# Router transposes placed behind ready products, and batch 1's preparation for the last feed-forward placed after the attention core

## The reference, cut to what matters

```python
x = x + _L0_xattn_ref(_layernorm(x), ctx_1024, ...)      # attention-free mixer, layer norm, MLP 256-1024-256, layer norm
x = x + _L0_ffn_ref(_layernorm(x), ...)                  # mixture of 64 experts, 8 per token, and 2 shared MLPs
x = x + _L1_xattn_ref(_layernorm(x), ctx_1024, ...)      # masked softmax attention, 16 heads of 16
x = x + _L1_ffn_ref(_layernorm(x), ...)                  # gelu MLP with sign weights times a mean magnitude

# inside _L0_ffn_ref
probs = jax.nn.softmax(xf @ router_w + router_b, axis=-1)
tw, ti = jax.lax.top_k(probs, K)
tw = tw / jnp.sum(tw, axis=-1, keepdims=True)
h = jax.nn.silu(xf @ W1 + B1) @ W2 + B2                  # for every expert, weighted by its tw
# inside _L1_ffn_ref, bw = alpha * sign(w)
h = jax.nn.gelu(jnp.einsum('bsd,hd->bsh', x, bw1) + b1, approximate=False)
out = jnp.einsum('bsh,dh->bsd', h, bw2) + b2
```

## Time and profile before

| | |
|---|---|
| median of 3 runs | 1220.96 us (1219.16 to 1221.37) |
| the profiled execution's own time | 1220.14 us |
| its span | 1218.15 us |
| PE busy | 1132.7 us, 93% |
| DVE busy | 885.5 us, 73% |
| ACT busy | 704.4 us, 58% |
| POOL busy | 348.0 us, 29% |
| chain that ended last, by engine | PE 27%, DVE 7%, issue 4%, ACT 3% |

### The profile page before, as it was taken

One profiled execution on the slowest core, in us unless ns is written; L12 is line 12 of the kernel. 1 busy time (PEld: TensorE's weight loads), 2 busy tenths in 40 slices (PEclk: granted clock), 3 DMA queues, 4 the chain that ended last, 5 costly groups with the idle time before them and its releaser, 6 DMA issues. The chain is left out here.

```text
span 1218.1 us, 19950 instructions
## 1 busy us (share of the span) xinstructions
PE 1132.7 (93%) x6928; PEld 987.9 (81%) x6928; DVE 885.5 (73%) x1656; ACT 704.4 (58%) x1066; POOL 348.0 (29%) x343
## 2 busy tenths in 40 slices
PE   4889998988889999999999999999999999989998
PEld 3678887877779999999999888788788788777877
DVE  6888859766756556556554445999999989998575
ACT  2233334665534444444443155988988988987755
POOL 1613211622614204204100074412613522333120
PEclk9999999998999999999999999999999999999999
DMA  9200000043334342343220032322321432310011
GB/s 326 69 1 1 1 1 2 11 133 74 66 103 127 112 138 101 110 137 103 95 93 3 6 110 78 110 86 64 109 75 54 135 108 75 98 41 7 13 35 40
DMA packets 69032, 92.88 MB, mean 76 GB/s; under 512 B 16081, under 2 KB 33233, under 8 KB 68817
## 3 DMA queue, kind: packets, MB, share of 16 engines
q1 hardware_dynamic: 67328, 89.67, 24.7%
q10 hardware_dynamic: 1616, 2.10, 0.5%
HBM read 80.45 MB, written 11.14 MB: 75 GB/s over the span
## 5 line engine op out<-in xcount | busy, mean ns | idle before, releaser
L2055 DVE CUSTOM_DVE_ANT_0 at_pr<-at_sc,at_mk 128x512 f32<-128x512 f32 x256 | 165.5, 684 | 24.2 <-PE at_sc L2290 23.6
L1959 ACT ACTIVATE at_pr<-at_pr,at_nmx 128x512 f32<-128x512 f32 x256 | 170.5, 717 | 17.5 <-DVE at_nmx L2055 17.1
L2200 DVE TENSOR_TENSOR W_1l<-at_pt,W_1h 128x1024 fp32r<-128x1024 f32 x128 | 155.9, 1218 | 5.8 <-ACT W_1h L1954 5.3
L1954 ACT ACTIVATE W_1h<-at_pt 128x1024 fp32r<-128x1024 f32 x128 | 130.8, 1022 | 30.9 <-PE at_o L2324 28.8
L2305 PE MATMUL at_pt<-ident,at_pr 128*128 128x128 f32 x1024 | 134.1, 274 | 14.7 <-DVE W_1l L2200 14.0
L2305 PEld LDWEIGHTS at_pt<-ident,at_pr 128*128 128x128 f32 x1024 | 114.1, 141 | 38.0 <-issue 17.1
L229 ACT ACTIVATE moe_hs<-moe_hid,cols 128x512 f32<-128x512 f32 x120 | 82.8, 690 | 100.3 <-PE moe_hid L114 99.4
L248 DVE TENSOR_TENSOR moe_hl<-moe_ms,moe_hh 128x512 fp32r<-128x512 f32 x104 | 80.4, 773 | 64.3 <-ACT moe_hh L221 64.3
L262 DVE TENSOR_TENSOR moe_ms<-moe_hs,gate 128x512 f32<-128x512 f32 x104 | 78.4, 753 | 57.9 <-ACT moe_hs L229 57.2
L221 ACT ACTIVATE moe_hh<-moe_ms 128x512 fp32r<-128x512 f32 x104 | 65.8, 632 | 94.5 <-DVE moe_ms L262 94.5
L2324 PE MATMUL at_o<-W_1h,at_vaug 128*128 128x512 f32 x256 | 111.6, 436 | 0.3 <-DVE W_1l L2200 0.3
(11 more groups left out here) (304 smaller groups left out, 3291.2 us busy)
## 6 DMA issues: line engine op xcount, KB each, us to landing
gate<-expert_weights SPq DMA_DIRECT2D x256, 128.0 KB, 3.0
w_stage<-in_ew SPq DMA_DIRECT2D x32, 256.0 KB, 4.4
at_kp<-at_heads SPq DMA_DIRECT2D x96, 64.0 KB, 2.7
at_qp<-at_heads SPq DMA_DIRECT2D x96, 64.0 KB, 2.8
w_stage<-in_mask SPq DMA_DIRECT2D x16, 256.0 KB, 3.4
at_rb<-at_recip SPq DMA_DIRECT2D x64, 64.0 KB, 2.0
w_stage<-in_w SPq DMA_DIRECT2D x8, 256.0 KB, 7.9
w_stage<-in_sw SPq DMA_DIRECT2D x8, 256.0 KB, 3.4
```

Of the source, the lines that this page charges most:

```text
L1954: act.activation(PH[0][:, n % 2, :], PT[n % 2][:, :, :].rearrange("p c q -> p (c q)"), ACT.Copy)\
L1959: act.activation(pr_of(t)[:, x, :], pr_of(t)[:, x, :], ACT.Exp, bias=nmx[:, t % 4, x:x + 1], scale=-1.0).then_inc(s["ex"], 1)
L2055: dve.tensor_tensor_reduce(pr_of(t)[:, x, :], SB[x][:, :], mk[u // 2 % 2][:, j, :], -float(HD) ** -0.5, 3.0e38, ALU.add, ALU.min, nmx[:, t ...
L2200: dve.tensor_tensor(PH[1][:, n % 2, :], PT[n % 2][:, :, :].rearrange("p c q -> p (c q)"), f(PH[0][:, n % 2, :]), ALU.subtract).then_inc(s[ ...
```

## The change

It moves instructions within the engines' streams; none is added or taken away. In early_phase: `turn(b)` goes from the end of step b + 2 to slot 0 of step b + 3, behind `hidden` and `output`; `logits` and `turn_logits` go behind `output`; `turn_weights` goes from behind `output` in slot 5 to between `hidden` and `output` in slot 6; at n = 24 `output(22)` comes ahead of `hidden(24)`; on ACT, `turn_high` and `weights` go behind `high` and `relu` of their slot. In attention_phase all of batch 1's preparation leaves unit 7 for slots 1, 4, 5 and 6 of unit 8 (POOL: steps 2 and 6), and in `spare_uses` its two transposes come behind the sums.

```diff
@@ early_phase, ACT
-                    if t == 0 and 4 <= i < B + EARLY:
-                        turn_high(i - 3)
                     if 1 <= n <= LAST:
                         high(n - 1)
-                    if t == 6 and i >= 3:
-                        weights(i - 3)
                     if n < LAST:
                         relu(n)
+                    if t == 6 and 3 <= i < B + EARLY:
+                        weights(i - 3)
+                    if t == 0 and 3 <= i < B + EARLY:
+                        turn_high(i - 3)
...
@@ early_phase, PE
+                    if n == FIRST - HT:
+                        output(n - 2)
                     if n < LAST:
                         hidden(n)
...
-                    if t == 0 and i == 3:
-                        turn(0)
+                    if t == 6 and 3 <= i < B + EARLY:
+                        turn_weights(i - 3)
+                    if 2 <= n < LAST + 2 and n != FIRST - HT:
+                        output(n - 2)
                     if 3 <= i < B + EARLY:
+                        if t == 0:
+                            turn(i - 3)
                         if t == 1:
                             logits(i - 3)
                         if t == 2:
                             turn_logits(i - 3)
-                    if 2 <= n < LAST + 2:
-                        output(n - 2)
...
-                    if 3 <= i < B + EARLY:
-                        if t == 5:
-                            turn_weights(i - 3)
-                        if t == 7:
-                            biases(i - 3)
-                    if t == 7 and 3 <= i <= B + 1:
-                        turn(i - 2)
+                    if 3 <= i < B + EARLY and t == 7:
+                        biases(i - 3)
@@ spare_uses
-            out += [("ft", 0), ("ft", 1), ("ft", 2), ("ft", 3), ("a1", 0), ("a2", 0)]
+            out += [("ft", 0), ("ft", 1), ("a1", 0), ("a2", 0)]
+        if u == UNITS:
+            out += [("ft", 2), ("ft", 3)]
@@ attention_phase, POOL
-                        if st in (2, 4):
-                            norm_pool(pool, nm, B + st // 2 - 1, g.power)
+                        if st == 2:
+                            norm_pool(pool, nm, B, g.power)
...
-                        if st in (10, 13):
-                            add_b2(st // 3 - 3)
-                    if u == UNITS and st == 10:
-                        norm_pool(pool, nm, B + 2, g.power)
+                        if st == 10:
+                            add_b2(0)
+                    if u == UNITS and st in (2, 10):
+                        norm_pool(pool, nm, B + 1 + st // 8, g.power)
+                    if u == UNITS and st == 6:
+                        add_b2(1)
@@ attention_phase, ACT and PE (the same line in both)
-                if k > HT and k % HT in (5, 6) and k // HT + 1 < B:
+                if k % HT in (5, 6) and k // HT + 1 < B:
                     ffn_turn(2 * (k // HT + 1) + k % HT - 5)
@@ attention_phase, DVE
-                if 2 <= b < B and k % HT == 1:
+                if b < B and k % HT == 1:
                     ffn_stats(b)
-                if 2 <= b < B and k % HT == 4:
+                if b < B and k % HT == 4:
                     ffn_apply(b)
-                    ffn_bias(b)
-                if 2 <= b < B and k % HT in (5, 6):
+                    if b >= 2:
+                        ffn_bias(b)
+                if b < B and k % HT in (5, 6):
                     ffn_low_turn(2 * b + k % HT - 5)
...
-                        if st in (0, 3):
-                            ffn_stats(st // 3)
-                        if st in (4, 5, 7, 8):
-                            ffn_low_turn(st - 4 if st < 7 else st - 5)
-                        if st in (2, 5):
-                            ffn_apply(st // 3)
+                        if st == 0:
+                            ffn_stats(0)
+                        if st in (4, 5):
+                            ffn_low_turn(st - 4)
+                        if st == 2:
+                            ffn_apply(0)
```

More of the change, by code:

```diff
@@ L821, in _ @@
                         high_group1(2 * t + 1)
-                    if t == 0 and i == 3:
-                        turn_high(0)
                     if t == 1 and i >= 3:
@@ L1944, in _ @@
                             query(0)
-                    if u == UNITS - 1 and st in (4, 5, 7, 8):
-                        ffn_turn(st - 4 if st < 7 else st - 5)
+                    if u == UNITS - 1 and st in (4, 5):
+                        ffn_turn(st - 4)
                     if u == 0 and st == 13:
@@ L2454, in _ @@
                     if u == UNITS - 1:
-                        if st in (3, 4, 6, 7):
-                            ffn_turn(st - 3 if st < 6 else st - 4)
+                        if st in (3, 4):
+                            ffn_turn(st - 3)
                         if st == 9:
```

## The result

The changed kernel takes 1214.74 us (median of 20 runs, 1212.05 to 1219.24) and the kernel before 1221.32 us beside it (20 runs, 1219.14 to 1229.50): a ratio of 0.9942, 95% interval 0.9928 to 0.9956. The medians differ by 6.6 us where 16 were forecast, and the new one is within the range of 1197 to 1216, but outside the forecast's own of 1200 to 1210.

A forecast was written before the change was run, and what follows sets the result against it. PE was held by the router's chain, and by DVE in attention's unit 7. 1220.14 - 13.6 (router) - 4.4 (unit 7) + 2.1 (last stage) = 1204.2, median 1205.0 us; range 1197 to 1216, the forecast's own 1200 to 1210.

The forecast's parts named there:

- The waits for xn: Sign in the router: PE's waits for xn shrink from 11.0 us to some 5, none above 2.5.
- rival 4: Router: four short waits replace one long one and the clock stays at 1.2 GHz; 25 us lost, 1230; chance 0.05.
- The clock term: Router: clock losses of 2.5 and 1.7 us behind the waits for xn are gone, 4.2 us won.
- unit 7: Attention's core: batch 1's preparation leaves DVE, where PE waits for DVE; 4.4 us won, bounds 3.0 and 5.2.
- the router: Sum of steps 3 to 6 at the kernel's start: 3.0 + 2.9 + 4.7 + 3.0 = 13.6 us won.
- That moves the whole next chain by 2.82 us less what is lost on the way: Router: hidden and output run while PE waits for xn, so logits come 2.82 us sooner; 0.65 us lost per batch.
- Step 3: Router: `output(22)` runs inside the wait, so the next hidden comes 3.0 us sooner, or 2.2 if the clock drops.
- Other queues: Router: SP's stores and gate loads and POOL's split of group 2 keep their distances; costed at nothing.
- step 6: Router's last step: 4.5 us, cut to 3.0 because POOL splits weights beside it and DVE is slower there.
- rival 1: Router: the chain only shifts, 1.4 us lost per batch and further f_hl waits; 6 us won, 1213; chance 0.17.
- the last stage: Last feed-forward: batch 1's moved work delays `invert(22)` by 2.0 us and PE by 2.1; bounds 0.7 and 6.
- the prediction's own sign of being wrong: xn(b) follows xn(b - 1) by more than 33 us, or the last stage grows by more than 4.

The follow-up runs named there:

- experiment 2: Kernel before with only batch 1's preparation moved (attention half), nothing of the router: 1223.54 us, ratio 1.0012.
- experiment 9: The kernel before itself, unchanged, run once more for a second profile: 1230.1 us in its single run.
- experiment 10: Kernel before with the FFN's weight sums 64 columns wide and nothing of the change: 1220.19 us, ratio 0.9996.
- experiment 7: Changed kernel with `turn_logits` ahead of `output` again in slot 2: 1213.76 us, ratio 0.9929.
- experiment 3: Changed kernel with POOL's add of the shared bias for batches 0 to 2 made one batch later: 1214.73 us, ratio 0.9941.
- experiment 8: Changed kernel with the five edits of experiments 3 to 7 together: 1204.30 us, ratio 0.9853.
- experiment 4: Changed kernel with b2 of batch 1 added on DVE at k = 6 instead of on POOL: 1214.16 us, ratio 0.9944.
- experiment 6: Changed kernel with the FFN's first weight sums 64 columns wide instead of two: 1211.78 us, ratio 0.9919.
- experiment 11: Changed kernel with four of the edits of experiment 8, the weight sums two columns wide again: 1207.67 us, ratio 0.9885.
- experiment 12: Kernel of experiment 8 again, on the same chip as experiment 11: 1204.14 us, ratio 0.9854.
- experiment 5: Changed kernel with DVE's last two reciprocals ahead of the FFN step of their slot: 1212.54 us, ratio 0.9917.
- the combination: Changed kernel with the edits of experiments 3 to 7 together: 1204.30 us, and 1204.14 us when repeated.

## Why the prediction was wrong

**Right: the waits that go, and the clock of the router.** The waits for xn were to shrink to some 5 us with none above 2.5: 4.8 and 1.6. Those for the weights fell below 2 in all, 1.8, and more f_hl waits came, up to 1.3 us. The granted clock behind the turns is no longer at the 1.2 GHz level (0.99 over the stretch), and rival 4 is ruled out. Each xn follows the one before by less than 33 us. The clock term, 4.2 us, is borne out in size by the 3.3 us of the estimate above. It was no matter of luck as a sum: from turn(0) to the experts the clock was 0.94 to 0.96 in the four traces with before's router (before and experiments 2, 9 and 10), and 1.00 in all ten with the new one. One reading under it was luck, though. The prediction holds, against rival 4, that a wait of 3.38 us left the clock at 1.00. In experiments 2 and 9 the same waits ahead of turn(1), 3.38 and 3.40 us, were followed by 0.83 over ten us. In experiment 2:

```profile
248.00:258.00 10.00, 9.96 (x51) 8.57 (x52) 5.07 (x8) 6.22 (x9) 2.51 (x2) 0.83 0.19 51
```

So what speaks against rival 4 is that the waits left are 1.6 us at most, and not that a wait of 3.38 us is harmless.

**Right: unit 7.** 4.4 us forecast, 4.45 measured, waits of 3.6 us left where I said about 3.

**Wrong by 5.7 us: the router, 7.9 us in place of 13.6.** The middle block begins 6.7 us sooner and not 13. The clock came nearly as forecast, so what failed is the waits: the step "That moves the whole next chain by 2.82 us less what is lost on the way". I took 0.65 us for the turn of the logits behind `output`, and only by way of `choose`. The trace shows two losses there: `choose` did wait 1.08 us for it, and PE's `output` at the start of an expert waits 0.6 to 1.6 us for DVE's add of the expert before, which the turn of the logits used to cover. Experiment 7 prices this place at 2.5 us over the steps. Step 3 shows the same error at once: the next `hidden` stands 0.85 us behind turn(0), as forecast, and so 3.0 us sooner than before, but turn(1) still waits for xn(1), which follows turn(0) only 1.6 us sooner, and 2.3 us of waits for f_hl stand ahead of it that before has not. The other failed step is in "Other queues": I looked at SP and at POOL's weight split and not at POOL's `add_sb2`, which starts with xn. With PE's work moved up to xn, DVE's low and gate now stand beside it; experiment 3 gets 1.9 us back in the trace (though not in its median), and the two edits together 5.0 of the 5.7 (experiment 8). My own count of a low half beside POOL, 1.82 us, was there to be used and I used it for the last stage, and in the router for the weight split of step 6 alone. The rest, 0.7 us net, lies in step 6 (36.9 against 35.8), where the last add has no gap to go to; that this is its cause was not tried.

This is rival 1, "the chain only shifts", in size (6 us in the router) and in half of its mechanism. I gave it 0.17 because the slots without router work seemed to let DVE catch up. They do, but the loss is paid before them.

**Wrong by 2.1 us: the last stage, 4.2 in place of 2.1.** More than 4 us was also the prediction's own sign of being wrong. The term was named, with `ffn_apply` ahead of `invert(22)`, and mis-sized: I handed the 2.0 us of lateness on one for one, "late by 2.1 us, by either road". The reciprocal is late by what I said, 13.6 us behind the FFN's first product (1146.14 less 1132.58) where it stood 11.5 behind it. But its way back has no fixed length: the loads that wait for the store to DRAM followed it by 3.4 us, in before by 1.4 (1149.71 to 1151.09), and so ACT held its own FFN work for 2.08 us, which PE met as 2.05. SP in after, then in experiment 7, and ACT there:

```profile
1146.41 0.31 SPq L1609 DMA_DIRECT2D at_recip<-at_rc  x1
1149.83 1.24 SPq L1619 DMA_DIRECT2D at_rb<-at_recip  x3
```

```profile
1141.61 0.31 SPq L1610 DMA_DIRECT2D at_recip<-at_rc  x1
1142.98 2.02 SPq L1620 DMA_DIRECT2D at_rb<-at_recip  x3
...
1148.16 0.63 ACT L1870 ACTIVATE at_hh<-at_hs 128x512 fp32r<-128x512 f32 x1 [0.95 <-POOL at_hs L1730]
```

The slow store is not the whole of it. Experiment 7 has the same last stage with a store of 1.4 us, ACT waits 0.95 us and PE 0.97 for f_hl, and the stage still takes 83.4 us, 3.2 more than before. With a store of 3.1 to 3.4 us and the clock at 1.00 behind PE's wait it takes 83.9 to 84.7 (experiments 3, 4 and 6). So by the one trace of experiment 7 the new order itself costs some 3.2 us in place of 2.1, and the slow store 0.5 to 1.3 more. In after, and in experiment 2 with its store of 1.4, PE's clock fell besides, to 0.66 over 5 us behind a wait of 2 us; both took 84.4. Which instruction makes 3.2 out of 2.1 was not tried alone: at k = 7, before any wait for the heads, ACT's activation already starts 2.0 us later behind the FFN's first product than in before (18.6 against 16.6 us), where my two terms up to there come to 1.4.

What goes with the slow store shows in the DMA records. In after and experiments 3, 4 and 6 a load of code (q8, one packet of 16 KB) starts 0.8 to 1.0 us behind the store's issue and the store takes 3.1 to 3.4 us; in experiments 2 and 7 it starts 1.2 and 1.6 us behind it, and in the other traces there is none in that time, and the store takes 1.4. For this store the match holds in all fourteen traces, but no run moved the load on purpose, and elsewhere in attention stores of this kind take 1.35 to 4.36 us in after with causes of their own. Moving two reciprocals takes the first store out of that moment and brings 2.4 us back against after, 1.4 against experiment 7. The b2 add beside the low halves, which I had weighed against it, shows nothing beyond the spread (experiment 4).

**Missing: the clock at the FFN's weight sums, about 3 us.** Nothing in the prediction names this place: its sum puts the clock behind the router at nothing, without a reason. The fall costs 3.2 us in the trace of after, and the wide sums give 3.5 in the medians of experiments 11 and 12; in the kernel before they give 0.5. The attention half alone comes out at +2.6 us in the medians, where its own terms (−4.4 and +4.2) make −0.2; that fits a loss of 3 there, though its interval (−0.9 to +3.7 us) holds 0 too. The router half alone has the fall in its trace too (3.3 us), and its gain of 5.8 lies between its steps' 8.0 and those less 3.3. Not every fall costs as much: in the traces of experiments 3, 5 and 7 it is about 1.5 us (core to FFN 385.7 to 385.8 us, 384.3 in experiment 6). Nine of the ten traces with two columns have the fall, all but the first of before, and none of the four with 64. What makes the changed kernels meet it more often isn't settled. The kernel before has one trace with the fall and one without, so that most of its runs kept the clock rests on experiment 10, and no run here shows why.

The sum of the three, 5.7 + 2.1 + 3, is 10.8 us, against 9.4 missing in the medians (16 less 6.6). The trace of after has 2.5 us more between experts and core, from a clock of 0.77 at the experts' start (345 to 360 us; in the same 15 us of before, 0.89); with the same code there, the other traces have 392.0 (experiment 6) to 395.8 us (experiment 4), and the second of before 395.7, so this is its execution's luck and not the change's.

## What to carry to other kernels

When work is moved up to the instant at which a chain's result appears, list every engine's instruction that starts at that same instant, the idle engines' too: a POOL add that cost nothing beside an idle DVE cost 2 us beside a busy one. A product moved out from under a wait also uncovers the next wait, so look for who is served by the time that it filled. And when an operation is put ahead of a small one whose result goes through DRAM and back, let the small one go first: two reciprocals of 0.2 us moved forward shortened the last stage by 1.4 to 2.7 us.

## What the hardware showed that I had not expected

- TensorE's granted clock fell to the 1.2 GHz level with no idle time at all: 32 instructions of 128x2, back to back for 4.2 us, were followed by 0.50. The same 32 at 128x64 took 3.68 us and kept 1.00. Columns that nobody reads cost nothing here; they won 3.5 us in the combination and 0.5 in the kernel before.
- VectorE instructions with a single SBUF tensor input slow beside POOL too; no run here tells whether these are in a 2-port perf mode. The four pieces of `ffn_apply`, 1.38 us in after, took 2.36 us in experiment 5, where POOL's scaling of the heads ran at 1142.71. In experiment 11 the same pair met the other way, 1.38 us for DVE and 2.12 for POOL in place of 1.26, and the last stage took 81.2 us, against 82.2 in experiments 8 and 12, where DVE was the slow one:

```profile
1141.76 2.36 DVE L2071 TENSOR_SCALAR f_xn<-x_res,at_mv,at_rstd 128x256 f32<-128x256 f32 x4
```

- An improvement seen in one trace can vanish in the medians and come back in a combination: experiment 3 gained nothing in 10 runs, and the combination that contains it has the shorter steps in three traces (experiments 8, 11 and 12).
